# TensorE's order inside a step: the second weighing of an earlier block is put ahead of the projection of q's first half

## The reference, cut to what matters

```
q, k, v = split(shift_tokens(x) @ Wqkv)            # 16 heads of 64 each
q, k = rotary(l2norm(q) * q_scale), rotary(l2norm(k) * k_scale)
sim  = q @ k.T * 8, masked to the window of 32 and the one before
x    = x + (softmax(sim) @ v) @ Wo
hg   = layernorm(shift_tokens(x)) @ W1 + b1;  a, gate = split(hg)
x    = x + (a * gelu(gate)) @ W2 + b2
```

## Time and profile before

| | |
|---|---|
| time, median of 3 (lowest, highest) | 1723.12 us (1721.3, 1727.1) |
| span of the profiled execution | 1725.8 us |
| PE busy | 1585.1 us (92%) |
| DVE busy | 1446.8 us (84%) |
| ACT busy | 1117.1 us (65%) |
| POOL busy | 1069.6 us (62%) |
| chain that ended last | PE 75%, issue 9%, DVE 5%, ACT 4%, POOL 2% |

### The profile page before, as it was taken

How to read it: one execution, slowest core, us unless ns; L and a number is a source line. 1 busy time by engine, 2 the same in 40 slices (tenths; PEclk the granted TensorE clock), 3 DMA queues, 4 the chain that set the end, 5 groups by cost and what they waited for, 6 DMA issues and landing times.

```text
span 1725.8 us, 77157 instructions
## 1 busy us (share of the span) xinstructions
PE 1585.1 (92%) x32762; PEld 1278.6 (74%) x32763; DVE 1446.8 (84%) x3173; ACT 1117.1 (65%) x2014; POOL 1069.6 (62%) x1040
## 2 busy tenths in 40 slices
PE   4569999899999998999999999999999999999987
PEld 2247877777878777778777788777777777877874
DVE  8978988888889887888888889888888888888862
ACT  4346776667667666677666666666766666776663
POOL 3656766666666665667566567476576575665640
PEclk8589999999999999999999999999999999999998
DMA  2111110201111211110211111211111111011110
GB/s 86 31 44 49 40 49 25 77 24 48 44 37 37 65 36 38 41 49 28 67 34 48 41 37 40 61 37 52 38 40 40 49 49 44 29 47 44 33 46 13
DMA packets 41084, 75.06 MB, mean 43 GB/s; under 512 B 9472, under 2 KB 22568, under 8 KB 40744
## 3 DMA queue, kind: packets, MB, share of 16 engines
q1 hardware_dynamic: 40744, 70.12, 14.0%
HBM read 20.08 MB, written 2.10 MB: 13 GB/s over the span
## 4 chain that ended last, share of the span: by engine, by line
PE 75%; issue 9%; DVE 5%; ACT 4%; POOL 2%; ACTq 0%; DVEq 0%; POOLq 0%
PE bank L1359 8%; PE bank L1328 8%; PE bank L1465 8%; PE bank L1396 8%; PE wide L1436 7%; PE bank L1330 7%; PE bank L1329 7%; PE bank L1451 5%; PE bank L1529 4%; PE bank L1414 3%; PE bank L1385 2%; PE bank L1514 2%; PE bank L1515 1%; PE bank L1516 1%; PE bank L1476 1%
## 5 line engine op out<-in xcount | busy, mean ns | idle before, releaser
L864 POOL TENSOR_TENSOR qk<-qk,rnorm 128x512 f32<-128x512 f32 x384 | 401.8, 1046 | 351.0 <-DVE rnorm L1017 351.0
L856 POOL TENSOR_TENSOR qk<-qk,qk_sin 128x512 f32<-128x512 f32 x384 | 492.3, 1282 | 174.6 <-DVE qk_sin L978 174.5
L1180 ACT ACTIVATE squares<-bank 128x512 f32<-128x512 f32 x384 | 229.5, 598 | 152.6 <-DVE qk_sin L978 152.6
L988 DVE TENSOR_REDUCE norm<-squares 128x8 f32<-128x512 f32 x384 | 258.4, 678 | 30.7 <-ACT squares L1180 28.5
L1328 PE MATMUL bank<-w_hi,xs_hi 128*128 128x512 f32 x576 | 264.3, 459 | 12.3 <-ACT squares L1180 7.0
L971 DVE TENSOR_TENSOR qk<-bank,tables 128x512 f32<-128x512 f32 x384 | 261.6, 681 | 9.4 <-PE bank L1330 9.2
L978 DVE TENSOR_TENSOR qk_sin<-bank,tables 128x512 f32<-128x512 f32 x384 | 261.1, 680 | 0.6 <-POOL qk L856 0.6
L1330 PE MATMUL bank<-w_hi,xs_lo 128*128 128x512 f32 x576 | 230.3, 400 | 0.9 <-issue 0.9
L1329 PE MATMUL bank<-w_lo,xs_hi 128*128 128x512 f32 x576 | 229.2, 398 | 1.2 <-issue 1.1
L1359 PE MATMUL bank<-ident,qk 128*128 128x128 f32 x1536 | 226.5, 278 | 3.3 <-POOL qk L864 1.5
L1359 PEld LDWEIGHTS bank<-ident,qk 128*128 128x128 f32 x1536 | 181.0, 142 | 43.5 <-issue 5.0
(11 more groups left out here) (181 smaller groups left out, 2735.8 us busy)
## 6 DMA issues: line engine op xcount, KB each, us to landing
v<-v SPq DMA_DIRECT2D x96, 390.0 KB, 3.5
v<-v SPq DMA_DIRECT2D x72, 130.0 KB, 3.7
w_raw<-in_L_ffn_Wqkv SPq DMA_DIRECT2D x36, 256.0 KB, 3.9
w_o_s<-in_L_ffn_Wo SPq DMA_DIRECT2D x6, 512.0 KB, 5.9
w_raw<-in_L_ffn_W SPq DMA_DIRECT2D x6, 341.0 KB, 4.2
mix_x_nat<-in_L_attn_x SPq DMA_DIRECT2D x4, 256.0 KB, 3.5
w_raw<-x_res_scratch SPq DMA_DIRECT2D x4, 256.0 KB, 3.5
out<-w_raw SPq DMA_DIRECT2D x4, 256.0 KB, 3.1
```

The source lines that it names most:

```text
L856: pool.tensor_tensor(qk[:, g % 2, c, :], qk[:, g % 2, c, :], qk_sin[:, (QK_CHUNKS * g + c) % SINES, :], ALU.add).then_inc(added[c], 1)
L864: pool.tensor_tensor(view, view, rnorm[:, g % 2, c * HPC:(c + 1) * HPC].unsqueeze(2) .to_broadcast([P, HPC, DH]), ALU.mult).then_inc(norme ...
L988: dve.tensor_reduce(norm2[:, c * HPC:(c + 1) * HPC], squares[:, c % 2, :].rearrange("p (h d) -> p h d", d=DH), AX.X, ALU.add).then_inc(sum ...
```

## The change

One line of TensorE's loop moves. `project(step, Q0)` stood right behind `project(step, V0)`; now it stands behind `weigh(step - 3, 1)`. So V0 is followed by the last `expand` in t = 1, by `centre` in t = 3, and else by the second weighing, and Q0 comes after all of these. In t = 0 it is ahead of `widen_rstd`. Nothing is added or removed, and no other engine's order is touched.

```diff
@@ for step in range(STEPS): (TensorE)
                 turn_qk(step - 2, 0, qk_taken[2], step - 1)
                 project(step, V0)
-                project(step, Q0)
                 if t == 1:
                     expand(item - 2, 2)
                 if step == BLOCKS + 3:
@@
                 if step == 0:
                     late_output()
                 weigh(step - 3, 1)
+                project(step, Q0)
                 if step == BLOCKS + 4:
                     keep_busy(8)
                 if t == 0:
```

## The result

The changed kernel takes 1780.7 us (median of 4, 1773.6 to 1786.4) where the kernel before takes 1723.0 beside it (median of 4, 1721.3 to 1727.1): a ratio of 1.031 [1.028, 1.034], or 58 us. The forecast was 1743, its range ended at 1768. The direction was right, the size was not. TensorE's clock is not the reason: the clock granted was 0.98, 0.99 and 1.00 of the full 2.4 GHz in three stretches of the steps before (91.5 to 600, to 1200, to 1636 us), and 0.98, 0.99 and 0.99 in such stretches after.

The account below looks back on a forecast made before the run. TensorE's queue, PE busy 92% of the span, was taken as the bound. Bare steps lose 32 us, shrinking holes return 14: 18, rounded up to 20, on 1723 gives 1743 us; range 1722 to 1768.

Parts of the forecast that it names:

- Q0 is 0.99 us late, the weighing 0.70 us early: Shift in TensorE's queue worked out for t = 2, with Q0 behind the second weighing; TensorE's own sum unchanged.
- the lateness of `rotate`: Delay of VectorE's `rotate(step, 0)` from late Q0: 0.63, 1.5, 0.66 and 1.66 us in t = 0 to 3.
- What TensorE loses at its first tight wait: Loss per step at K1 or the scores' start: 0.55, 1.0, 0.2 and 0.65 us in t = 0 to 3.
- Which steps lose: Only bare steps, without a hole in the scores, lose: 16, 16, 11 and 8 of them, 32 us.
- The hole covers the lateness: In steps with a hole in the scores, mean 0.94 us, it covers losses of 0.2 to 1.0 us.
- What the holes may give back: Earlier block requests shrink the scores' holes: 9 us in t = 2, 5 in t = 3, together -14.
- a block is asked for a fixed number of instructions earlier: Assumption on TensorE's instruction fetch: a request inside the weighing goes out 0.70 us earlier and shrinks the hole as much.
- What could cover it: The weighing's wait for `o_normed[0]` behind V0: 0.55 us left, costed at nothing; otherwise another 10 to 20 us.
- D: Rival: VectorE becomes the bound and every step pays as a bare one, 58 us; 1780 or more, chance 0.1.
- C: Rival: losses as worked out and holes in the scores that don't shrink; 1756 us, chance 0.22.

Follow-up runs that it names:

- run 5: Kernel before plus 64 small matmuls in step 2; one execution, 1742.9 us. The place meant is 193 modulo 256 in TensorE's instruction count.
- Run 2: Q0 moved in t = 2 alone, with VectorE's `normalise` put ahead of `rotate` there; 1727.6 against 1721.4 us for the kernel before, ratio 1.0038.
- runs 3 and 8: Q0 moved in t=1 (3) or t=1 and t=3 (8), `normalise` (t=1: also `gate`) ahead of `rotate`; 1718.6 against 1721.4, 1722.8 against 1724.1 us.
- run 4: Kernel before with an unread 128x512 VectorE reduction ahead of `rotate(step, 0)` in every step, TensorE's order untouched; 1743.5 against 1721.4 us.

## Why the prediction was wrong, step by step

- **"Q0 is 0.99 us late, the weighing 0.70 us early", and the lateness of `rotate`: right.** Four steps give 0.65, 0.67, 1.64 and 1.63 for 0.66, 0.63, 1.5 and 1.66. The waits of `rotate` come to 101.9 us in 91 waits for a forecast of 106 in some 90.
- **"What TensorE loses at its first tight wait": right in sum, wrong in place for t = 0, 2 and 3.** I took K1 for the tight wait. In t = 0 TensorE waits for `scale_xn` at the mask instead, 22 times, and for `squares` before K1 once, as before. K1 did come 0.19 late in t = 2, as worked out. But the maxima stand in the same VectorE queue, and `merge_heads` waits for the first `shift` behind them: 0.47 for 0.2, and 0.93 for 0.65, in the two steps shown. In t = 1 `expand` stood behind Q0 and now waits 0.33 for `gate(item - 2, 1)`, so the mask is 1.22 late for 1.0. That the sum comes to 31 us for 32 all the same is luck: the slips in the price are made up by fewer steps being bare, by six bare steps of t = 0 that lose nothing, and by one that loses 3.67.
- **"Which steps lose": the step that failed.** "The hole covers the lateness" was argued from the mean of a hole, 0.94 us. The 10, 10 and 14 holed steps of t = 0, 1 and 2 lost 0.78, 1.08 and 0.72 on average, as much as bare ones or nearly. Only t = 3 was covered (+0.09), and there one step's gain of 2.39 makes the mean. In t = 0 and 1 the wait comes ahead of the scores, and the long holes (some 2 us) were still there behind it. Six of t = 1 went, most of them short, but two others, 0.45 and 0.43 us long in before, are 2.4 and 2.2 long in after: the block ahead of them takes 1.7 and 0.95 us longer to run, but the transfer that they wait for starts 3.3 and 2.9 us later after that block's start. The mean hid that: there are short holes, which cover less than the loss, and long ones, which stay.
- **"What the holes may give back", -14: failed.** The gaps over 0.15 us at the place of run 5, on every line, hold 73.4 us, 69.6 before. In t = 2, where 9 us were to come back, the scores' holes went from 16.4 to 19.1 and the weighing got 11 new ones, 5.7 us. Run 2 shows that the order of TensorE opens the holes in the weighing, without VectorE late; the scores' holes hold 15.8 us in it, so their growth is not shown to come of the order. The assumption that failed is that a block is asked for a fixed number of instructions earlier: in the kernel before, nine tenths of the transfers start 65 to 254 instructions ahead of their block. I asked where the request for a block would lie and did not ask the other question: what the move does to the places in the stream that had no hole. Q0 stood between the weighing at the end of one step and that at the beginning of the next; V0 alone is left between them. So in the 11 weighings the place is reached 0.60 to 0.68 us sooner after its block's start, while the transfer starts no sooner (in the median 2.28 us after that start, 2.26 before). In the scores behind them it is the other way round: the block is longer by 0.5 to 0.7 us, with Q0 in it, but the transfers start later too (1.85 us for 1.34), and the gaps hold 12.2 us for 10.6. Holes are smaller in the profiles of runs 3 and 8, in t = 1 and 3, where `expand` and `centre` still stand between.
- **"What could cover it", nothing for `o_normed[0]`: nothing seen.** The weighing starts 0.88 us into the step in t = 2, right behind V0, and no wait for VectorE's `o_normed[0]` is put down to it there.
- **The rivals.** The time is that of D (1780 or more), and D's arithmetic, every step paying as a bare one (58 us), comes near what the table's steps show in sum (61 us), in part by luck, as three steps whose holes grew make up 10 us of it. But D's reason was not the one: VectorE is busy 81% and still waits 42.2 us for the scores, so it has not become the bound. It is late at one place of a step, and TensorE waits for what stands there. I gave D 0.1, and C, which kept the holes as they were, 0.22; C, like my forecast, leaves out that a hole and a late queue add up.

Two things stay open. One is what makes a block's transfer start late, and so the same boundary cost 0.4 us in one kernel and 2.2 or 2.4 in the next; TensorE's order alone is not the reason, since one of the two boundaries of t = 1 costs 2.2 us in run 4 too, where no instruction of TensorE moved. The other is how much of the difference between two profiles' holes is the change and how much the execution, since each kernel has one trace.

## What to carry to other kernels

Moving an instruction back in a full queue makes everything late that stands behind its reader; follow that reader's whole queue to each wait of the bounding engine, and price the tightest one, not the first. Don't credit a hole with covering a delay unless its own timeline shows that the hole would have ended when it did. Where the consumer's order can be fitted to the producer's, do both in one change: in t = 1 that alone was worth 23 us. And look at single steps before trusting a mean that agrees with a forecast.

## What was not expected of the hardware

- TensorE's long idle times without a releaser lie mostly at one place in every 256 of its instructions, most of them in runs of short matmuls, and end 1.2 to 1.6 us after the transfer of the next block has ended; all lines taken together, 61 such gaps hold 65 us of the kernel before, 4% of the span. The Trainium skill ("Runtime: NRT & Kernel Launch", "Instruction fetch mechanics") gives blocks of 256 instructions, which agrees, and says that crossing one is mostly hidden, which these 65 us do not bear out.
- Such a gap can be opened by order alone: the 64 short matmuls of the second weighing ran through in every t = 2 step of the kernel before, and stopped in 11 of 24 once three long matmuls no longer stood ahead of them (in 10 with VectorE's order fitted, run 2).
